# A relational graph layer with residual norm on one core: x without a scale, adjacency units loaded in pairs

## What is computed

```python
masks = (relation[None] == rel_ids[:, None, None, None]).astype(x.dtype)   # relation is adj
h = jnp.einsum('rbnm,bmd->rbnd', masks, x)
y = jnp.einsum('rbnd,rdo->bno', h, weight) + bias
out = _layernorm(x + y)          # over the 128 features, eps 1e-5
```

## Time and profile before

| What | Value |
|---|---|
| Median of three runs | 124.0 us |
| The profiled execution | 124.87 us, of which span 123.1 us |
| Busy in the span: TensorE matmul, VectorE, ScalarE, GpSimd | 106.7, 96.5, 87.4, 73.3 us |
| Mean of what the DMA engines moved | 343 GB/s (42.23 MB) |
| Mean granted TensorE clock | 0.968 of full speed |

### The profile page before, as it was taken

One profiled execution on the slowest core, in us unless ns is written; L12 is line 12 of the kernel. 1 busy time (PEld: TensorE's weight loads), 2 busy tenths in 40 slices (PEclk: granted clock), 3 DMA queues, 4 the chain that ended last, 5 costly groups with the idle time before them and its releaser, 6 DMA issues.

```text
span 123.1 us, 2783 instructions
## 1 busy us (share of the span) xinstructions
PE 106.7 (87%) x960; PEld 76.2 (62%) x974; DVE 96.5 (78%) x321; ACT 87.4 (71%) x106; POOL 73.3 (60%) x87
## 2 busy tenths in 40 slices
PE   6989992999599999999999999999999999999000
PEld 2369662768367676767676767676767677698000
DVE  1684736852998989899988998799969998798830
ACT  4098870999578949894989498949894989533310
POOL 2016000991293997399739983989398939809310
PEclk9999999999999999999999999999999999999755
DMA  4999999999999999999999999999999991040441
GB/s 124 361 362 414 414 405 410 407 390 430 407 416 387 420 418 397 415 418 421 404 408 418 418 415 375 432 426 418 384 428 426 421 359 46 0 170 0 170 156 33
DMA packets 12851, 42.23 MB, mean 343 GB/s; under 512 B 929, under 2 KB 7202, under 8 KB 9762
## 3 DMA queue, kind: packets, MB, share of 16 engines
q1 hardware_dynamic: 10432, 38.87, 79.5%
q10 hardware_dynamic: 2402, 3.15, 6.9%
HBM read 37.81 MB, written 4.19 MB: 341 GB/s over the span
## 4 chain that ended last, share of the span: by engine, by line
PE 64%; DMA 14%; SPq 9%; DVE 6%; issue 2%; ACT 0%; DVEq 0%
PE h_ps L591 36%; PE ids_t L577 17%; DMA x_sb<-x 14%; PE y_ps L605 10%; SPq L383 8%; DVE mask_t L690 2%; DVE row_max L666 1%; DVE rows L699 1%; DVE stats L705 1%; SPq L380 1%; PE ids_t L605 1%; DVE rows L744 0%; SPq L400 0%; DVE moments L711 0%; ACT std L506 0%
## 5 line engine op out<-in xcount | busy, mean ns | idle before, releaser
L489 ACT ACTIVATE junk<-adj_sb,minus 128x2048 bf16<-128x2048 int32 x32 | 63.8, 1995 | 1.4 <-issue 0.8
L690 DVE TENSOR_SCALAR mask_t<-ids_t,down 128x1024 bf16<-128x1024 uint16 x64 | 47.5, 743 | 7.8 <-PE ids_t L577 7.3
L577 PEld LDWEIGHTS ids_t<-ident,adj_sb 128*128 128x128 bf16 x512 | 36.9, 123 | 17.3 <-DMA adj_sb<-adj 4.7
L577 PE MATMUL ids_t<-ident,adj_sb 128*128 128x128 bf16 x512 | 40.3, 222 | 3.2 <-DMA adj_sb<-adj 3.1
L458 POOL TENSOR_SCALAR rows<-rows,rstd,shift 128x128 f32<-128x128 f32 x59 | 25.6, 451 | 17.8 <-DVE shift L737 17.8
L591 PE MATMUL h_ps<-mask_t,x_lo 128*128 128x512 bf16 (+2 forms) x160 | 33.4, 336 | 0.1
L591 PE MATMUL h_ps<-mask_t,x_hi 128*128 128x512 bf16 (+2 forms) x146 | 30.4, 332 | 2.4 <-DVE mask_t L690 1.3
L450 POOL TENSOR_TENSOR x_sb<-x_sb,bias_sb 128x1024 f32<-128x1024 f32 x8 | 19.0, 2377 | 7.4 <-DVE x_lo L750 7.3
L435 POOL TENSOR_TENSOR x_up<-x_sb,up 128x1024 f32<-128x1024 f32 x7 | 13.3, 1899 | 16.2 <-DVE up L684 16.1
L502 ACT ACTIVATE h_all<-h_ps 128x512 f32<-128x512 f32 (+2 forms) x20 | 10.2, 508 | 15.4 <-PE h_ps L591 15.4
L591 PEld LDWEIGHTS h_ps<-mask_t,x_hi 128*128 128x128 f16 x160 | 13.2, 98 | 9.2 <-DVE mask_t L690 2.2
(11 more groups left out here) (42 smaller groups left out, 33.3 us busy)
## 6 DMA issues: line engine op xcount, KB each, us to landing
adj_sb<-adj SPq DMA_DIRECT2D x24, 1024.0 KB, 20.4
adj_sb<-adj SPq DMA_DIRECT2D x16, 512.0 KB, 10.4
x_sb<-x SPq DMA_DIRECT2D x8, 512.0 KB, 18.7
out<-rows ACTq DMA_DIRECT2D x6, 512.0 KB, 7.4
out<-rows SPq DMA_DIRECT2D x1, 512.0 KB, 2.9
out<-rows SPq DMA_DIRECT2D x2, 256.0 KB, 3.7
w_sb<-weight SPq DMA_DIRECT2D x1, 64.0 KB, 5.7
bias_row<-bias ACTq DMA_DIRECT2D x1, 0.5 KB
```

Of the source, the lines that this page charges most:

```text
L489: nc.scalar.activation(junk[:, at % 2], adj_sb[:, slot, 2 * k:2 * k + 2, :], ACT.Square, scale=2.0, bias=minus[:, 0:1], accum_out=squares[ ...
L577: last = nc.tensor.transpose(bank[:, j, :], words[:, j // step(b), j % step(b), 0, :], ident[:, :])
L690: nc.vector.tensor_scalar(mask_t[:, b % 2, :, u * P:(u + 1) * P], ids_t[u % T_BANKS][:, :, :].bitcast(UINT16), down[:, b:b + 1], None, ALU ...
```

## The change

It does away with the scale: x_hi is x rounded to f16, x_lo the rest, the masks hold 1.0. The row maxima are still taken, now from x_hi of the batch in work and used only by the test at the end (largest below 2^15, least not below 2^-3). In batch 0 x is split in two halves, by ScalarE and VectorE, each with its own semaphore. All units but the first two of batch 0 are loaded in pairs of 1 MB; unit 0 is loaded before x of batch 0, and x of batch 1 before all units of batch 1. ScalarE's checks of batches 0 to 3 are spread anew over the groups (`pairs_checked_by`), and there are 6 and 2 idle turns in place of 9 and 1. The groups stay as they were. Cut to what matters (left out: names of semaphores and tiles, and the bodies of functions that go, which stand in the listing above):

```diff
+LEAST = 2.0 ** -3
+MOST = 2.0 ** 15
...
+    def alone(b, u):
+
+        return b == 0 and u < 2
+
     def loads_of(b, k):
-
-        return 16 * (b // ADJ_SLOTS + (1 if b % ADJ_SLOTS >= EARLY else 0))
+        return 16 * len([c for c in range(b % ADJ_SLOTS, b + 1, ADJ_SLOTS) if not alone(c, 2 * k)])
+
+    def pairs_checked_by(g):
+
+        first = [1, 2, 2, 4, 6, 8, 11, 13]
+        if g.index < len(first):
+            return first[g.index]
+        return min(PAIRS * (g.b + 1) + (2 if ends_batch(g) else 0), PAIRS * B)
...
+            load_unit(0, 0)
             load_x(0)
-            load_unit(0, 0)
             load_unit(0, 1)
             sp.dma_start(w_sb[:, 0, :], weight[0]).then_inc(s_w, 16)
-            for u in range(2, J):
-                load_unit(0, u)
-            load_unit(1, 0)
+            for k in range(1, PAIRS):
+                load_adj(0, k)
             load_x(1)
-            for u in range(1, J):
-                load_unit(1, u)
+            for k in range(PAIRS):
+                load_adj(1, k)
             load_x(2)
...
-            def scale_x(b):
...
-                pool.wait_ge(s_up, b)
                 pool.wait_ge(s_hi, b + 1)
                 if b >= 2:
                     pool.wait_ge(s_prod, last_group_of(b - 2) + 1)
-                nc.gpsimd.tensor_tensor(x_lo[:, b % 2], x_up[:, :], x_hi[:, b % 2],
+                nc.gpsimd.tensor_tensor(x_lo[:, b % 2], x_sb[:, b % X_SLOTS], x_hi[:, b % 2],
                                         ALU.subtract).then_inc(s_lo, 1)
...
-                scale_x(b + 1)
...
-                if b < EARLY:
+                if alone(b, 2 * k):
...
-            def split_hi(b):
-                act.wait_ge(s_scale, b + 1)
+            def split_hi(b, js, signal):
+                act.wait_ge(s_x[b % X_SLOTS], 16 * (b // X_SLOTS + 1))
                 if b >= 2:
                     act.wait_ge(s_prod, last_group_of(b - 2) + 1)
-                nc.scalar.activation(x_hi[:, b % 2], x_sb[:, b % X_SLOTS], ACT.Copy,
-                                     scale=up[:, b:b + 1]).then_inc(s_hi, 1)
+                    act.wait_ge(s_rm, b - 1)
+                nc.scalar.activation(x_hi[:, b % 2, js], x_sb[:, b % X_SLOTS, js], ACT.Copy).then_inc(signal, 1)
...
-            act.wait_ge(s_const, 1)
-            split_hi(0)
+            split_hi(0, slice(0, HALF), s_hi0)
+            split_hi(0, slice(HALF, J), s_hi)
             act.wait_ge(s_spread, 1)
             nc.scalar.activation(bias_sb[:, :], y_ps[:, 0, :], ACT.Copy).then_inc(s_biased, 1)
+            act.wait_ge(s_const, 1)
             check(0, 0)
-            for g in groups[:LAST]:
+            for g in groups[1:LAST]:
                 b = g.b
-                if g.index >= 1:
-                    copy_h(groups[g.index - 1])
-                if g.index == 0:
-                    continue
-                if g.index == 1:
-                    check(0, 1)
-                elif not ends_batch(g):
-                    check(b, 2)
-                    check(b, 3)
-                else:
-                    split_hi(b + 1)
+                copy_h(groups[g.index - 1])
+                if ends_batch(g):
+                    split_hi(b + 1, slice(0, J), s_hi)
                     if b >= 2:
                         store(sets[b - 2])
-                    check(b + 1, 0)
-                    if b >= 1:
-                        root(sets[b - 1])
-                    check(b + 1, 1)
+                todo = range(pairs_checked_by(groups[g.index - 1]), pairs_checked_by(g))
+                for n, at in enumerate(todo):
+                    check(at // PAIRS, at % PAIRS)
+                    q = groups[g.index - 2] if g.index >= 2 else None
+                    if n == 0 and q and ends_batch(q):
+                        root(sets[q.b])
             a, c, e, d = groups[LAST:]
             copy_h(groups[LAST - 1])
-            check(a.b, 2)
-            check(a.b, 3)
+            for at in range(pairs_checked_by(groups[LAST - 1]), pairs_checked_by(a)):
+                check(a.b, at % PAIRS)
...
-                    pe.wait_ge(s_hi, g.b + 1)
+                    if g.index:
+                        pe.wait_ge(s_hi, g.b + 1)
...
-                if lo <= J < hi:
+                if lo <= J < hi and g.index:
                     pe.wait_ge(s_lo, g.b + 1)
                 for j, part in todo[lo:hi]:
+
+                    if g.index == 0 and j % HALF == 0:
+                        pe.wait_ge(((s_hi0, s_hi) if part is x_hi else (s_lo0, s_lo))[j // HALF], 1)
...
-            idle_turns(9)
+            idle_turns(6)
...
-            idle_turns(1)
+            idle_turns(2)
...
-            def scale_maxima(b):
-                slot = b % X_SLOTS
-                dve.wait_ge(s_x[slot], 16 * (b // X_SLOTS + 1))
-                nc.vector.tensor_reduce(row_max[:, b, :], x_sb[:, slot], AX.X, ALU.max,
+            def row_maxima(b):
+                dve.wait_ge(s_hi, b + 1)
+                nc.vector.tensor_reduce(row_max[:, b, :], x_hi[:, b % 2], AX.X, ALU.max,
                                         apply_absolute_value=True).then_inc(s_rm, 1)
...
-            def scale_largest(b):
...
-            def scale_up(b):
...
-                                        down[:, b:b + 1], None, ALU.mult).then_inc(s_mask, 1)
+                                        1.0, None, ALU.mult).then_inc(s_mask, 1)
...
+            def split_lo(b, js, hi, lo):
+                dve.wait_ge(hi, 1)
+                nc.vector.tensor_tensor(x_lo[:, b % 2, js], x_sb[:, b % X_SLOTS, js], x_hi[:, b % 2, js],
+                                        ALU.subtract).then_inc(lo, 1)
...
+                dve.wait_ge(s_rm, B)
+                nc.vector.tensor_reduce(odd[:, 0:1], row_max[:, :, :], AX.XY, ALU.max).then_inc(s_odd, 1)
+                nc.vector.tensor_reduce(odd[:, 1:2], row_max[:, :, :], AX.XY, ALU.min).then_inc(s_odd, 1)
+                dve.wait_ge(s_odd, 2)
+                nc.vector.tensor_scalar(high[:, :], odd[:, 0:1], MOST, None, ALU.is_ge).then_inc(s_high, 1)
+                dve.wait_ge(s_high, 1)
+                nc.vector.scalar_tensor_tensor(out=worst[:, :], in0=odd[:, 1:2], scalar=LEAST, in1=high[:, :],
...
+                nc.vector.tensor_reduce(odd[:, 2:3], squares[:, :], AX.X, ALU.max).then_inc(s_odd, 1)
+                dve.wait_ge(s_odd, 3)
...
+                nc.vector.scalar_tensor_tensor(out=found[:, :], in0=odd[:, 2:3], scalar=2.0 * N + 4.0, in1=worst[:, :],
+                                               op0=ALU.is_gt, op1=ALU.max).then_inc(s_found, 1)
...
-            for part in (scale_maxima, scale_largest, scale_power, scale_down, scale_up):
-                part(0)
             mask_unit(0, 0)
-            split_lo(0)
+            split_lo(0, slice(0, HALF), s_hi0, s_lo0)
+            split_lo(0, slice(HALF, J), s_hi, s_lo)
 
             for g in groups[:LAST]:
                 n = groups[g.index + 1]
 
...
-                due = g.b + 1 if ends_batch(n) and g.b + 1 < B else None
-                early = due is not None and due > 1
                 if q:
                     sum_rows(q)
                 mask_unit(n.b, n.units[0])
                 if q:
                     statistics(q)
-                if early:
-                    scale_maxima(due)
+                if g.place == (2 if g.b == 0 else 0):
+                    row_maxima(g.b)
                 if n.count > 1:
                     mask_unit(n.b, n.units[1])
                 if r:
                     combine(r, q)
-                if early:
-                    scale_largest(due)
-                    scale_power(due)
                 if n.count == GU:
                     mask_unit(n.b, n.units[2])
-                if early:
-                    scale_down(due)
-                    scale_up(due)
                 if r:
                     invert(r)
                     other_root(r)
@@ -816,9 +780,6 @@
                     add_roots(r)
                     invert_sum(r)
                     shift_rows(r)
-                if due == 1:
-                    for part in (scale_maxima, scale_largest, scale_power, scale_down, scale_up):
-                        part(due)
 
             last, a, c, e, d = groups[LAST - 1:]
             r, ra, rb = sets[B - 2:]
@@ -826,12 +787,13 @@
             sum_rows(q)
             mask_unit(a.b, GU)
             statistics(q)
+            row_maxima(a.b)
             mask_unit(a.b, GU + 1)
             sum_rows(last)
+            statistics(last)
             mask_unit(a.b, GU + 2)
-            statistics(last)
+            combine(r, last)
             mask_unit(a.b, GU + 3)
-            combine(r, last)
             find_far()
             find()
             for part in (invert, other_root, add_roots, invert_sum, shift_rows):
```

More of the change, by code:

```diff
@@ L46, in adj_resnorm_kernel @@
     EARLY = 2
+    HALF = J // 2
     PAIRS = J // 2
@@ L130, in adj_resnorm_kernel @@
         x_sb = sb("x_sb", [P, X_SLOTS, J, D], FP32)
```

(24 more changed lines are left out.)

44 lines of the change are left out of this document (7 added, 37 removed).

## The result

The changed kernel takes **125.62 us** (median of four runs, 124.88 to 126.17), the kernel before 124.01 in the same comparison (123.67 to 124.12): a ratio of 1.0131, 95% interval 1.0074 to 1.0188. It is slower, by 1.6 us, and above the range of the prediction. The profiled execution took 125.48 us, its span is 123.7.

What follows compares the result with a forecast made beforehand. TensorE sets the pace from 34 to 95.7 us, with DMA full too. Gains of 0.35 + 0.4 + 0.2 = 0.95 us less 0.44 in the tail give 0.51, so 123.5 us from 124.0; range 122.9 to 125.2.

Steps and rivals of the forecast that it cites:

- the clock falls in the hole before the pair: Rival, before batch 1's first pair: TensorE idles, one or two steps run at half rate, 1.3 to 2.6 us; 125.3, chance 0.15.
- the sum: Whole kernel: TensorE 0.95 us ahead at the 17th group, less 0.44 lost in the tail, makes 0.51 us less.
- The scale at no cost: Steady stage: removing the scale's multiplications on GpSimd and small operations on VectorE is worth nothing by itself.
- the stall at 29.87: VectorE's 2.65 us wait for x in batch 2's row maxima goes, since they read the f16 half in work.
- the hole at 95.67: TensorE's 0.24 us hole late in the steady stage nearly all goes, with VectorE's 91.89 stall: 0.2 us gained.
- the sixth group: TensorE's products there start at 33.1 us (32.9 to 33.5) in place of 33.86.
- the packet of instructions: Near batch 1's first pair: the 16 KB packet should come behind the pair, leaving TensorE 1.5 us idle.
- the next pair: Batch 1's second pair of units, arriving at about 23.2 us, then sets the time for TensorE.
- it decides once the idle time exceeds what the trace shows to be harmless, 2.35 us: Before batch 1's pair: TensorE's clock falling matters only if its idle time exceeds the 2.35 us seen before.
- The tail: VectorE, first mask to first test: batch 7's maxima add 1.14 us, 0.70 of idle goes; 0.44 us lost.
- the masks, assumed the same: VectorE's masks with a constant stay at 0.74 us (0.6 to 0.8), four of them in the tail.
- ScalarE's late checks: Steady stage: later 2.0 us checks make ScalarE late by about 0.4, taken up; cost nothing, at worst 1 us.

Runs made afterwards that it cites:

- experiment 1: Changed kernel with eleven matmuls on zeros before the transposes of batch 1's first unit, where TensorE had idled; 123.24 us, ratio 0.9925 to the kernel before.
- experiment 3: Changed kernel with x of batch 1 loaded behind batch 1's first pair, not ahead of it; 123.15 us, ratio 0.9907 to the kernel before.
- experiment 10: Changed kernel with five matmuls on zeros, in place of eleven, in TensorE's hole before batch 1's first unit; 123.22 us, ratio 0.9936 to the kernel before.
- experiment 4: Kernel before with one edit, x of batch 1 loaded ahead of unit 0 of batch 1; 124.76 us, ratio 1.0002 to the kernel before.
- experiment 7: Experiment 3 with the row maxima of batch 7 left out, the test covering seven batches; 122.51 us, ratio 0.988 to the kernel before.
- experiment 8: Experiment 3 with the row maxima of batch 7 taken one group earlier on VectorE, nothing left out; 122.72 us, ratio 0.9888 to the kernel before.
- experiment 12: Experiment 3 without the second, general pass (five branches and their code, never taken here); 121.65 us, ratio 0.9812 to the kernel before.
- experiment 11: Changed kernel with single 512 KB unit loads again, x of batch 1 still ahead of unit 0; 124.03 us, ratio 0.998 to the kernel before.
- experiment 6: Kernel before with nine matmuls into a free bank in its own 2.35 us hole, ahead of batch 1's unit 1; 124.74 us, ratio 1.0056.
- experiment 9: Kernel before with x of batch 1 loaded ahead of batch 1, and its units 0 and 1 as one 1 MB load; 125.98 us, ratio 1.0093.

## Why the prediction was wrong

**What holds.** The rival "the clock falls in the hole before the pair" is what happened: its mechanism, its place and, for one step, its size (1.3 us, with a time of 124.8; measured 1.43 us between 102.51 and 101.08). Take it away, as experiments 1, 3 and 10 do, and the sum stands: TensorE 1.0 to 1.15 us ahead at the tail's first mask (101.08, 101.00 and 100.94 against 102.09) where 0.95 was forecast, and 123.15 to 123.24 us where 123.5 was. The scale at no cost, the stall at 29.87 and the hole at 95.67 came out as written. Two things came out by luck. The measured 125.62 lies near that rival's 125.3, but one step was lost to the clock and not up to two; 0.9 us of it lies at the end of the span, of which the prediction says nothing. And the sixth group, with the clock held, starts at 32.83 where 33.1 was forecast, but not by the way forecast: the packet of instructions did not move behind the pair, the pair was taken up only 0.79 us earlier than unit 1 before (19.95 against 20.74), and from there TensorE ran without waiting for the next pair, which was to set the time.

**The step that failed** is "Against it: the packet of instructions that I expect to move, which would leave an idle time of 1.5 us", and with it the chance of 0.15. The packet is expected behind the pair, because TensorE would take up unit 0 only later. It came ahead of it: a packet of 16 KB started at 17.61 us and held one DMA engine for 1.10 us. The DMA queues of the changed kernel from 17.5 to 18.2 us (packets, MB, share of 16 engines) answer to the earlier trace rows:

```profile
q8 instruction: 1, 0.02, 9.8%
```

Fifteen engines were through with their parts of the pair between 18.00 and 18.63, the last at 19.90, and TensorE took the pair up at 19.95, when the last was through. So the idle time was 2.66 us. The packet does not wait for TensorE to take up that unit: in 13 of the 14 profiles it starts between 16.44 and 17.83 us, while TensorE takes up unit 0 anywhere from 16.76 to 20.26 (in experiment 4 it starts at 20.60). Where it does fall behind the first pair, as in experiments 7, 8 and 12, the pair is taken up at 17.63 to 17.78. The pair at 19.9 was still within what the prediction allowed (19.4 to 20.7): for the arrival it had a range, for the idle time it took the best end.

**The second fault** is "it decides once the idle time exceeds what the trace shows to be harmless, 2.35 us". One harmless hole is no limit: the clock fell after 2.08 (experiment 11), 2.47, 2.66 and 2.84 us, and held in the profile of the kernel before after 2.35, with other work ahead of it. In about one in eight of that kernel's executions even that hole may not have been harmless (experiment 6). The Trainium skill, page TensorE: Matmul & The Clock Gate, section HAM oscillation, describes idle time from DMA waits between bursts as what throttles TensorE. The traces here agree, with waits of 2.08 to 2.84 us where the page's example has about 3 to 5, and the page's warning was worth more than the single row that I set against it.

**The tail** was mis-sized. Forecast 0.44 us lost, measured 0.06 gained. The maxima took the 1.20 us of a float32 reduction, as said: an f16 input is no faster (mean 1203 ns on the page, 1217 before), which is what the Trainium skill, page VectorE: DVE Perf Modes, section on the perf-mode tier table, states. But the masks, assumed the same, are quicker now that they take a constant and not a column of scalars:

```profile
L664 DVE TENSOR_SCALAR mask_t<-ids_t 128x1024 bf16<-128x1024 uint16 x64 | 43.4, 687 | 23.4 <-PE ids_t L566 22.6
...
L657 DVE TENSOR_REDUCE row_max<-x_hi 128x8 f32<-128x1024 f16 x8 | 9.6, 1203 | 0.0
```

They take 687 ns against 743, about 0.2 us for the four of the tail. From the mask at 102.51 to the first test at 108.83 it is 6.32 us, only 0.11 more than before, where 0.44 was forecast; the statistics and the sum behind the maxima found their inputs waiting. The tests take 0.93 us (108.83 to 109.76), 0.17 less. The maxima are not free, though: experiments 7 and 8 give 0.66 and 0.84 us for taking them off the tail.

**Right:** ScalarE's late checks cost nothing. In the steady stage, from 34 to 96 us, ScalarE waited for TensorE's products for 8.6 us in 9 waits, against 10.1 in ten before:

```profile
ACT h_all L496 <- PE h_ps L584: 8.6, 9, 1.8
```

VectorE waited for its root by 0.4 us at the longest, and TensorE never waited for ScalarE.

**What is open.** Against experiment 1 the changed kernel is 2.38 us slower by the medians. The fall of the clock is 1.43 of it; 0.9 lies behind the last normalisation (6.06 against 5.2 us in the profiles), where instruction packets and the last stores share the DMA engines. (The two medians are of different sets; between the two profiled executions it is 2.28 us.) What decides how many packets fall there was not found. That most of the long executions of the kernel before have the same source is likely (experiment 6 ended 4.7 us after its last normalisation in a run of 123.68 us, the kernel before 5.8 us after it in one of 124.87), but it was only argued. What, besides the length of a hole, decides whether the clock falls in it is open too: the work ahead of it and the moment were never varied one at a time.

## What to carry to other kernels

When a load is made larger or moved, write down what TensorE does between the last work that it has and that load's **last** engine, and treat any new hole near 2 us as a fall of the clock until a profile shows otherwise; a fall costs about a step (1.4 us here), more than the larger loads gain (about 0.3). The cure is the order of the loads, or a few matmuls on zeros behind the last real work. If a range is given for an arrival, carry the whole range into the mechanism that it can set off, not its favourable end.

## What the runs showed of the hardware that was not expected

- After a thinned stage the clock fell with 2.08, 2.47, 2.66 and 2.84 us of idle before batch 1, and was held with 1.34 and 1.49, and, behind some of batch 1's work, with 1.36, 1.65, 1.73, 1.83 and 2.35. Each time it was at half for 3.4 us, from 0.1 us before the work came back to 1.0 us after it: nearly all the harm falls on useful work.
- One packet of 16 KB of instructions on one DMA engine (1.10 us in mid-stream, up to 2.6 us beside the last stores of experiment 9) makes one engine of 16 late, and every load behind it in the queue stays that late: in the changed kernel the first and the last engine end 0.6 us apart for x of batch 1 (15.51 and 16.14) and 1.9 us apart for each of the loads that follow.
- Leaving out the code behind a branch that is not taken saved 1.2 to 1.5 us at the end of the kernel (experiment 12 against 3).
